# Last attention batch of a two-layer transformer kernel: order of score units, value products and router logits, and fewer products of constants

## The reference

```python
x = layernorm(x + attn0(x))                       # 16 heads, head width 8, rotary embedding
x = layernorm(x + ffn0(x))                        # 8 experts; softmax(x @ Ws + bs), each expert takes its 256 top tokens
x = layernorm(x + attn1(x))                       # keys and values from a latent of width 32
x = layernorm(x + ffn1(x))                        # 16 experts, each token takes 4:
logits = -sum((x[:, None] - keys)**2, -1) + x @ rw.T + rb
```

## Time and profile before

| | us |
|---|---|
| median of 3 runs | 701.9 (702.34, 697.56, 701.9) |
| span of the profiled execution, first to last instruction | 625.5 |
| median less that span | 76.4 |
| last attention batch and logits, layer 0 | from 139.4 to 168.4 of the span |
| the same, layer 1 | from 390.8 to 421.2 |

### The profile page before, as it was taken

The page is one execution under the profiler, slowest core; times in us unless marked ns, Lnnn a source line. Parts: engine busy times, 40 slices in busy tenths (PEclk is TensorE's granted clock), DMA queues, the critical chain, the costliest instruction groups (busy, mean ns, idle before and its releaser), DMA issues.

```text
span 625.5 us, 16615 instructions
## 1 busy us (share of the span) xinstructions
PE 541.5 (87%) x5152; PEld 382.4 (61%) x5152; DVE 438.8 (70%) x1591; ACT 418.0 (67%) x1111; POOL 322.7 (52%) x429
## 2 busy tenths in 40 slices
PE   5579999999967995279999999987999999999960
PEld 2134444545755895244455544665899999999960
DVE  5478888994486521756799999497887788743275
ACT  2138888886261564163888988732778888899834
POOL 2675666506001678465144430646566777777740
PEclk9559999999999999575999999999999999999975
DMA  6602090002100225409405000102122211211363
GB/s 194 171 25 78 12 276 3 2 2 51 21 4 4 49 48 99 146 22 273 145 10 144 3 2 2 51 19 45 49 55 54 63 59 59 60 59 58 100 202 122
DMA packets 54649, 44.42 MB, mean 71 GB/s; under 512 B 15155, under 2 KB 45123, under 8 KB 54438
## 3 DMA queue, kind: packets, MB, share of 16 engines
q1 hardware_dynamic: 47302, 31.75, 17.6%
q0 software_dynamic: 7264, 11.62, 7.2%
HBM read 29.91 MB, written 11.87 MB: 67 GB/s over the span
## 4 chain that ended last, share of the span: by engine, by line
PE 67%; DVE 11%; DMA 5%; ACT 5%; issue 5%; SPq 3%; POOL 2%; DVEq 0%; ACTq 0%; POOLq 0%
PE bank L1321 11%; PE bank L1331 10%; PE bank L905 10%; PE bank L888 7%; PE bank L870 5%; PE bank L922 3%; ACT prob L1464 2%; PE bank L1116 2%; DVE W L1964 2%; PE bank L1128 2%; PE bank L946 2%; DMA sum<-rt,idx_s 1%; PE bank L1011 1%; PE bank L930 1%; DMA prob<-xs,idx_g 1%
## 5 line engine op out<-in xcount | busy, mean ns | idle before, releaser
L1771 DVE TENSOR_REDUCE mx<-bank 128x2 f32<-128x512 f32 x256 | 163.4, 686 | 38.2 <-PE bank L870 36.4
L1464 ACT ACTIVATE prob<-bank 128x512 f32<-128x512 f32 x256 | 142.1, 601 | 36.0 <-PE bank L888 31.2
L1650 ACT ACTIVATE queries<-bank,prob 128x128 f32<-128x128 f32 x316 | 90.1, 368 | 19.5 <-PE bank L1321 16.3
L1321 PE MATMUL bank<-keys,prob 128*128 x632 | 85.5, 279 | 0.7 <-issue 0.5
L1331 PE MATMUL bank<-W,queries 128*128 x632 | 84.4, 277 | 0.0
L870 PE MATMUL bank<-keys,queries 32*128 32x256 f16 x512 | 77.9, 293 | 4.2 <-DVE mx L1771 2.0
L905 PE MATMUL bank<-prob,augs 128*32 128x256 f32 x1024 | 79.0, 393 | 0.0
L1321 PEld LDWEIGHTS bank<-keys,prob 128*128 128x128 f32 x632 | 76.8, 192 | 3.4 <-issue 2.1
L784 POOL DMA_INDIRECT prob<-xs,idx_g x64 | 61.8, 966 | 32.6 <-DVE idx_g L2175 15.5
L1331 PEld LDWEIGHTS bank<-W,queries 128*128 128x128 f32 x632 | 76.7, 192 | 1.9 <-issue 0.5
L793 POOL DMA_INDIRECT parts<-augs,idx_s x64 | 63.0, 985 | 20.5 <-issue 8.9
(11 more groups left out here) (296 smaller groups left out, 1035.8 us busy)
## 6 DMA issues: line engine op xcount, KB each, us to landing
W<-in_w SPq DMA_DIRECT2D x48, 256.0 KB, 3.8
sum<-zero SPq DMA_DIRECT2D x3, 1024.0 KB, 9.8
xr<-XT SPq DMA_DIRECT2D x12, 128.0 KB, 2.0
xs<-X SPq DMA_DIRECT2D x2, 768.0 KB, 5.5
prob<-xs,idx_g POOLq DMA_INDIRECT x80, 2.6
XB<-sum SPq DMA_DIRECT2D x1, 1024.0 KB, 5.3
Y<-sum SPq DMA_DIRECT2D x4, 256.0 KB, 4.7
W<-sum SPq DMA_DIRECT2D x4, 256.0 KB, 5.4
```

What stands on the lines that cost most here:

```text
L1321: last = nc.tensor.matmul(bank[2 + p % 2][:, P * f:P * f + P], wc[:, p % 4, P * f:P * f + P], xsT2[:, bass.ds(at, 1), :], start=True, stop ...
L1464: nc.scalar.activation(prob[:, v % 8, :, :], st_bank(b, v)[:, :], ACT.Exp, scale=SCALE).then_inc(exp_done, 1)
L1650: last = nc.scalar.activation(hid2[:, p % 4, f, :], bank[2 + p % 2][:, P * f:P * f + P], ACT.Gelu, bias=wc[:, p % 4, WB + f:WB + f + 1])
L1771: nc.vector.tensor_reduce(m_at, bank[S1B[u % 2]][:, :].rearrange("p (j k) -> p j k", j=2), AX.X, ALU.max).then_inc(s1_used, 1)
```

## The change

In the last batch PE's order is written anew: score units go in pairs, two ahead of the products with values; the turns of the normed tiles come later, and the logits of tiles 0 to 11 (`tail_logits(0)` to `(2)`) come behind the last exponential instead of between the score units. DVE's and ACT's orders follow. The products of constants of this part go from 64 to 17 a layer (hold 10+4+6+6 to 8; fill 5+5+16+12 to 3+6). The removed functions `tail_turns`, `tail_before` and `tail_after` only held the old order.

```diff
@@ pe_last_soft @@
                 av(lay, b, par, 3, 1)
                 for v in range(4):
                     st(lay, c, nxt, v)
-                tail_turns(lay, i, 2)
-                hold(lay, 10)
-                bt(lay, b, 1)
+                if lay == 1:
+                    keys_squared()
+                hold(lay, 8)
                 st(lay, c, nxt, 4)
                 st(lay, c, nxt, 5)
-                hold(lay, 4)
+                bt(lay, b, 1)
+                st(lay, c, nxt, 6)
+                st(lay, c, nxt, 7)
                 av(lay, c, nxt, 0, 0)
-                st(lay, c, nxt, 6)
                 av(lay, c, nxt, 0, 1)
-                st(lay, c, nxt, 7)
+                st(lay, c, nxt, 8)
+                st(lay, c, nxt, 9)
                 out_transposes(lay, b)
-                st(lay, c, nxt, 8)
-                tail_turns(lay, i, 7)
-                st(lay, c, nxt, 9)
+                st(lay, c, nxt, 10)
+                st(lay, c, nxt, 11)
+                av(lay, c, nxt, 1, 0)
+                av(lay, c, nxt, 1, 1)
                 out_product(lay, b)
-                av(lay, c, nxt, 1, 0)
-                st(lay, c, nxt, 10)
-                av(lay, c, nxt, 1, 1)
-                st(lay, c, nxt, 11)
-                tail_turns(lay, i, 10)
                 st(lay, c, nxt, 12)
                 st(lay, c, nxt, 13)
-                hold(lay, 6)
-                tail_turns(lay, i, 13)
+                tail_turn(lay, 0)
+                st(lay, c, nxt, 14)
+                st(lay, c, nxt, 15)
+                av(lay, c, nxt, 2, 0)
+                av(lay, c, nxt, 2, 1)
                 bt(lay, c, 0)
-                av(lay, c, nxt, 2, 0)
-                st(lay, c, nxt, 14)
-                av(lay, c, nxt, 2, 1)
-                st(lay, c, nxt, 15)
+                tail_turn(lay, 1)
@@ pe_last_tail @@
+                c, par = NB - 1, 1
+                av(lay, c, par, 3, 0)
+                av(lay, c, par, 3, 1)
+                tail_turn(lay, 2)
+                fill(3)
+                bt(lay, c, 1)
+                tail_logits(lay, 0)
+                out_transposes(lay, c)
+                tail_turn(lay, 3)
+                out_product(lay, c)
+                tail_logits(lay, 1)
+                tail_logits(lay, 2)
+                tail_logits(lay, 3)
+                fill(6)
@@ behind pe_last_tail @@
-                fill(12)
                 tail_turn(lay, 4)
                 fill(4)
                 tail_logits(lay, 4)
@@ act_last @@
-                exps(lay, i - 1, range(9, 14))
+                exps(lay, i - 1, range(9, 12))
                 ot_evac(lay, i - 1, 0)
-                exps(lay, i - 1, (14, 15))
+                exps(lay, i - 1, range(12, 16))
                 ot_evac(lay, i - 1, 1)
@@ DVE @@
+            def dve_last(lay):
+
+                b, c = NB - 2, NB - 1
+                norm(lay, b, 0)
+                tail_variance(lay, 0)
+                tail_scale(lay, 0)
+                if lay == 1:
+                    dve.wait_ge(ksq_done, 1)
+                    nc.vector.tensor_tensor(br1[:, :], rb[:, :], bank[M6][:, 0:E1], ALU.subtract).then_inc(br_ready, 1)
+                norm(lay, b, 1)
+                output_added(lay, b)
+                output_statistics(lay, b)
+                tail_variance(lay, 1)
+                tail_evac(lay, 0)
+                norm(lay, c, 0)
+                tail_evac(lay, 1)
+                tail_scale(lay, 1)
+                tail_evac(lay, 2)
+                norm(lay, c, 1)
+                if lay == 1:
+                    dve.wait_ge(xsq_ready, 1)
+                    step(nc.vector.tensor_reduce(xn2[:, 0:EARLY], xsq[:, 0:EARLY, :], AX.X, ALU.add))
+                tail_evac(lay, 3)
+                output_added(lay, c)
+                output_statistics(lay, c)
+                tail_variance(lay, 2)
+                if lay == 0:
+                    soft_logits(0)
+                else:
+                    choice_scores(0)
+                tail_scale(lay, 2)
+                if lay == 0:
+                    soft_scaled(0)
+                else:
+                    choice_taken(0, EARLY)
+                    choice_written(0)
+                tail_evac(lay, 4)
```

More of the change, by code:

```diff
@@ L1072, in pe_last_tail @@
-                fill(16)
+                c, par = NB - 1, 1
[12 more added lines that the diff above has]
+                fill(6)
@@ L1179, in tail_logits, with keys_squared @@
                     last.then_inc(lg_done, 1)
[L1181 to L1202, removed]
+            def keys_squared():
+                pe.wait_ge(wr_ready, 2)
+                nc.tensor.matmul(bank[M6][:, 0:E1], ones[:, :], ksq[:, :], start=True,
+                                 stop=True).then_inc(ksq_done, 1)
             def join_turn(c):
@@ L1790, in dve_iteration @@
                     output_statistics(lay, i - 2)
[L1792 to L1803, removed]
-                    tail_after(lay, i, u)
-                    if u == 15 and i == NB:
-                        norm(lay, i - 1, 0)
+            def dve_last(lay):
[34 more added lines that the diff above has]
+                tail_evac(lay, 4)
             def q_evac(lay, b, par):
@@ L1851, in tail_evac @@
                 nc.vector.tensor_copy(XT[:, P * t0:P * t1], bank[M6][:, 0:P * (t1 - t0)]).then_inc(xt_ready, 1)
-            def tail_before(lay, i, u):
-                if i == NB and u == 0:
-                    tail_variance(lay, 0)
-                    tail_scale(lay, 0)
-                    if lay == 1:
-                        dve.wait_ge(ksq_done, 1)
-                        nc.vector.tensor_tensor(br1[:, :], rb[:, :], bank[M6][:, 0:E1], ALU.subtract).then_inc(br_ready, 1)
-                if i == NB and u == 7:
-                    tail_evac(lay, 0)
-                if i == NB + 1 and u == 4:
-                    tail_evac(lay, 3)
-            def tail_after(lay, i, u):
-                if i == NB and u == 11:
-                    tail_evac(lay, 1)
-                    tail_variance(lay, 1)
-                    tail_scale(lay, 1)
-                    tail_evac(lay, 2)
-                    if lay == 1:
-                        dve.wait_ge(xsq_ready, 1)
-                        step(nc.vector.tensor_reduce(xn2[:, 0:EARLY], xsq[:, 0:EARLY, :], AX.X, ALU.add))
-                if i == NB + 1 and u == 4:
-                    if lay == 0:
-                        soft_logits(0)
-                    else:
-                        choice_scores(0)
-                if i == NB + 1 and u == 11:
-                    tail_variance(lay, 2)
-                    if lay == 0:
-                        soft_scaled(0)
-                    else:
-                        choice_taken(0, 8)
-                    tail_scale(lay, 2)
-                    if lay == 1:
-                        choice_taken(8, EARLY)
-                        choice_written(0)
-                    tail_evac(lay, 4)
             def join_statistics(n):
@@ L2312, in _ @@
                                                    op0=ALU.mult, op1=ALU.add).then_inc(wr_ready, 1)
-                dve_last(lay, NB)
-                dve_last(lay, NB + 1)
+                dve_last(lay)
                 if lay == 0:
```

## The result

The changed kernel took 689.5 us (median of 4 runs, 688.44 to 691.75) beside 702.12 for the kernel before in the same comparison (4 runs, 697.56 to 703.46). The ratio is 0.984, 95% interval 0.981 to 0.988: 8.6 to 13.4 us less. The forecast was 692.4, in a range of 689 to 699. The profiled execution after has a span of 688.6 us and a time of 690.45, so a time is its span and 1.85 us.

The account below looks back on a forecast made before the run. The prediction took the PE chain up to the start of `tail_logits(4)` as the bound, with DVE work also limiting layer 1. Gains 6.3 + 4.1 - 0.9 = 9.5 us gave 701.9 - 9.5 = 692.4, range 689 to 699.

Parts of the forecast that it names:

- Gain there as a gain in the whole: Start of `tail_logits(4)`, 167.78 and 420.61 in the two layers: all later work hangs on it, so its gain counts fully.
- Layer 0, 6.3 us: Layer 0, last batch: logits 4 start at 161.5 against 167.78, gain 6.3 us, bounds 5.4 and 6.8.
- ACT's term: Layer 0: 14 exponentials at 0.56 each, two copies 0.76 and 0.04 end exponential 15 at 152.4 against 158.04.
- the sum for PE, 152.1: Layer 0: PE's work from 144.49, 7.4 us and 0.2 for unit 7, ready at 152.1, 0.3 before ACT.
- rival 2: PE falls behind ACT, costing 1.5 us a layer plus a later start of squares: gain 6, 696 us; chance 0.1.
- 0.4 for `soft_logits(0)`: Layer 0, DVE between variance and `tail_scale(2)`: `soft_logits(0)`, about 0.85 us, costs 0.4 beyond POOL's root.
- pairing makes the second unit free: Score units on PE: a pair takes 0.40 us, next work 0.33 behind its start, a single unit 0.39.
- Layer 1, 4.1 us: Layer 1, last batch: logits 4 start at 416.45 against 420.61, gain 4.1 us, bounds 3.3 and 4.6.
- The clock, 0.9 us in layer 1: Layer 1: granted clock falls, 19 constants behind logits 4 take up to 4.1 us instead of 2.1; cost 0.9, between 0 and 4.
- the gap from 412.0 on: Layer 1, PE from 412.0 to 416.45: some 0.9 us of work in 4.4, so the clock was expected to fall.
- The slower rival: Clock falls in layer 0 and stays low through the threshold search's ten rounds: 4.3 us slower, 706; chance 0.05.
- The 76.4 us between span and median are not touched: Whole kernel: span goes from 625.5 to 616.0, the 76.4 us between span and median stay in the forecast.

Follow-up runs that it names:

- single units: Changed kernel with units 6 to 15 of the last batch single again between value products, moved logits and 17 constants kept; 629.3 us beside 629.59 for before, one run each.
- third profile: Changed kernel, unchanged, timed and profiled a third time on another chip; 692.64 us beside 700.89 for before, ratio 0.988.
- fewer constants behind: Changed kernel with 9 instead of 18 constants behind the last logits of layer 0, 8 instead of 19 in layer 1; 619.64 us.
- evacuation placed first: Changed kernel with `tail_evac(4)` directly behind `tail_scale(2)`, ahead of `soft_scaled(0)` and `choice_taken(0)`; 618.2 us beside 629.59 for before, one run each.

## Why the prediction was right

- **What decides.** "Gain there as a gain in the whole": the stages gained 10.07 us up to the gathers, and the whole 8.6 to 13.4. On the quick chip, with one run each, three variants of the changed kernel took 9.95 to 11.39 less than before.
- **Layer 0, 6.3 us.** Measured 6.44. The limit up to the last exponential was not the one I had. Exponentials follow at (3.57 - 0.60)/6 = 0.50, not 0.56, so ACT was done 0.9 earlier, counted from the units, than I had it. PE was the limit instead: its timeline lists no idle from 142.63 to the output product at 157.00, and the last value products began at 152.91, 0.66 behind exponential 15. That is 10.28 behind the units; the sum for PE, 152.1, lay 10.2 behind them, so it was right, and because it was only 0.3 under ACT's, the error in ACT's term did no harm. It is rival 2's event at no price, and that the two sums lay so close is luck. Behind it the prediction charged 0.4 for `soft_logits(0)` beyond POOL's root, and 0.10 was measured.
- **What order is worth.** The single units show what I had as one part among several: with them 4.42 of the 6.44 go, about 1.5 of it through the clock. The mechanism in the prediction (pairing makes the second unit free, 0.33 us) holds in the rows; its indirect worth, ACT fed and PE without a pause, was about twice what I had worked out ahead of that run (2.9 without the clock's share, against 1.2 to 1.6).
- **Layer 1, 4.1 us.** Measured 4.21, and nearly all markers hold: `tail_scale(1)` 1.93 for 1.7, `choice_scores(0)` at once behind variance and logits 2. The Trainium skill, GPSIMD Engine Reference, section Key points, has GpSimd contend with VectorE instructions in a two-port mode or with two SBUF inputs; the runs agree that `tail_scale(1)` contends with the squares (0.60 alone, 1.93 and 3.02 beside them), and do not show which of the two conditions it meets.
- **The clock, 0.9 us in layer 1, nothing in layer 0.** This step failed in its places, not in its sum. "Layer 0 has no such gap: 0.3 us before turn 4 is the longest" is true of the pause (0.33), and yet the clock fell there, by which up to the first gather 0.57 us came back (3.16 in the third profile, 1.35 of it by its second fall). In layer 1 it fell at 410.1, 411.6 of the old time scale, and not in the gap from 412.0 on that was the reason given: PE's timeline lists no pause from 406.91 to there. Other executions paid there, 0.94 in the third profile and 1.53 in that with fewer constants behind. The constants behind the last logits did stretch to 4.21 as said, but cost nothing up to the gather (9.78 against 9.77), probably because the gather hangs on POOL's counts and their DMA, which the evacuation placed first bears out. The slow turn and the four slow constants ahead of the logits are in the 4.21 already.
- **The slower rival** had the right event, the fall in layer 0, and the wrong course: the clock came back within 3 to 7 us behind the constants and search steps, and did not stay low through the search.
- **The time around the span.** "The 76.4 us between span and median are not touched" was wrong as a picture: there are 1.85 us around it. The other 70 or so lie inside later stages and go with the chip. The forecast was unharmed because the gain is about the same in microseconds on both kinds of chip.

## What to carry to other kernels

Work out an order by its limiting engine, but expect the worth of keeping that engine fed to be larger than the time of the instructions rearranged: one late unit delays the copy behind it, and this the next products. Constants are free only in a wait, and there only while the clock is up, so an order and its constants have to be changed together; here the order alone kept 5.9 of 10.1 us and fewer constants alone gave nothing. Before an evacuation is moved up to bring one chain forward, look at who waits for the work that it overtakes.

## What the runs showed of the hardware that was not expected

The granted clock fell to 1.2 GHz while PE was nearly always busy: in the first profile after, PE is counted busy for all of 157 to 160 and the clock is half from 160.9. What stands ahead of each fall around turn 4 of layer 0 is the run of 20 logits with 8 columns each, 2.30 us. That this run brings it down is not shown. With the 28 constants behind it the clock stayed up, and with nine behind it, it stayed up in one profile and fell in another. In layer 1 of the changed kernel the clock fell 2.7, 1.8 and 0.7 us behind the start of the run in three profiles, and at its start in the profile with fewer constants behind. The low stretch there was 10 to 14 us long. In layer 1 the kernel before, too, had a fall in one of its two profiles. So what sets it stays open. The price was nothing to 1.5 us ahead of the last logits, and nothing to 3.2 us behind them.

One program took 629.6 us on one chip and 700.2 to 703.3 on others, with equal times in the two stages changed here and 68 us more in the stage of gathers and pairs. Engines wait there for up to 5.4 us, in part for releasers that the profile doesn't show. The cause was not tried and stays open.
